# A vision tower on one core: padding copies, one weight load, PSUM bank sets and idle matmuls between the token rounds and the expert tiles

## The reference, cut to what matters

```
h   = tok(x, log_dt, B_ri, inv_A_real, A_imag)        # (16, 256, 512), complex exponentials, einsum
h   = concat(cls_tok, h)                              # (16, 257, 512)
u   = layernorm(layernorm(h)) ; gates = u @ W_in + b_in
s_t = (1-a_t) s_{t-1} + a_t b_t ; y = s * tanh(c)     # a = sigmoid(delta), scan over tokens
h   = h + y @ W_out + b_out + layernorm(h) @ W_skip + b_skip
x3  = layernorm(h)
scores = softmax(x3 @ gate_w) ; top 2 of 8 experts, weights comb
routed = sum_e comb_e * ((silu(x3 @ w_gate_e) * (x3 @ w_up_e)) @ w_down_e)      # hidden size 352
shared = (silu(x3 @ sw_gate) * (x3 @ sw_up)) @ sw_down                          # hidden size 704
h   = h + routed + shared
```

## Time and profile before

| | |
|---|---|
| median of 3 runs | 1160.75 us (1159.69 to 1163.04) |
| profiled execution, its own time | 1161.9 us |
| span in that execution | 1160.2 us |
| PE busy | 1068.6 us, 92% of the span |
| DVE, ACT, POOL busy | 812.9, 346.8, 381.5 us |
| mean granted PE clock | 0.968 |

### The profile page before, as it was taken

The page is one execution under the profiler, slowest core; times in us unless marked ns, Lnnn a source line. Parts: engine busy times, 40 slices in busy tenths (PEclk is TensorE's granted clock), DMA queues, the critical chain, the costliest instruction groups (busy, mean ns, idle before and its releaser), DMA issues.

```text
span 1160.2 us, 26590 instructions
## 1 busy us (share of the span) xinstructions
PE 1068.6 (92%) x7943; PEld 697.8 (60%) x7944; DVE 812.9 (70%) x2124; ACT 346.8 (30%) x659; POOL 381.5 (33%) x352
## 2 busy tenths in 40 slices
PE   3187899999999999999999998799999999999994
PEld 3055657766776677767776676355555555555552
DVE  7988998899889988898889655444444444444442
ACT  4422442344334443443334331111111111111110
POOL 1010132023212321232113211155555555655564
PEclk9588998999999999999999999899999999999998
DMA  8443445455553555455555985599999877787875
GB/s 288 132 149 102 123 119 173 129 149 161 177 166 110 166 176 159 122 157 182 155 139 148 287 285 189 135 181 200 178 201 165 135 127 132 133 131 129 134 120 75
DMA packets 305135, 183.32 MB, mean 158 GB/s; under 512 B 256098, under 2 KB 274914, under 8 KB 302900
## 3 DMA queue, kind: packets, MB, share of 16 engines
q1 hardware_dynamic: 288324, 136.38, 47.1%
q0 software_dynamic: 15504, 36.46, 15.7%
q10 hardware_dynamic: 1248, 9.72, 2.4%
HBM read 55.36 MB, written 79.47 MB: 116 GB/s over the span
## 4 chain that ended last, share of the span: by engine, by line
PE 75%; DVE 5%; DMA 4%; issue 2%; SPq 1%; ACT 1%; POOL 0%; POOLq 0%; DVEq 0%; ACTq 0%
PE bank L1001 28%; PE bank L1165 11%; PE bank L1175 11%; PE bank L1166 11%; PE bank L1080 7%; PE bank L1015 4%; DMA wexp<-x3w 1%; PE bank L1068 1%; PE bank L1084 1%; DMA x_slots<-x3w,sl 1%; DMA wexp<-w_halves 1%; DVE wexp L1381 1%; PE bank L1067 0%; PE bank L1066 0%; PE bank L1065 0%
## 5 line engine op out<-in xcount | busy, mean ns | idle before, releaser
L1001 PE MATMUL bank<-wexp 128*128 128x256 f16 (+2 forms) x3252 | 407.3, 286 | 10.4 <-issue 5.9
L1001 PEld LDWEIGHTS bank<-wexp 128*128 128x128 f16 x3252 | 310.5, 99 | 90.9 <-issue 16.0
L1165 PE MATMUL bank<-wexp,rows_in 128*128 x852 | 257.7, 315 | 10.8 <-issue 6.7
L1166 PE MATMUL bank<-wexp,rows_in 128*128 x852 | 257.3, 315 | 0.0
L1733 DVE SCALAR_TENSOR_TENSOR mixed<-bank,mixed 128x352 f32<-128x352 f32 x71 | 37.2, 524 | 163.4 <-ACT mixed L1338 160.7
L979 POOL DMA_INDIRECT out<-x2w,rows_in x70 | 111.8, 1597 | 119.4 <-DMA out<-x2w,rows_in 90.0
L933 POOL TENSOR_TENSOR inv<-var,power 128x4 f32<-128x4 f32 x17 | 29.2, 1715 | 362.1 <-DVE var L1563 362.1
L967 POOL TENSOR_TENSOR ex<-base,ld 128x8 f32<-128x8 f32 x71 | 120.7, 1700 | 76.1 <-DVE ld L1711 50.1
L1165 PEld LDWEIGHTS bank<-wexp,rows_in 128*128 128x128 f16 x852 | 83.6, 98 | 69.8 <-issue 28.8
L1338 ACT ACTIVATE mixed<-bank 128x352 f32<-128x352 f32 x71 | 32.9, 463 | 299.3 <-PE bank L1166 299.3
L1175 PE MATMUL bank<-wexp,gates 128*128 (+1 forms) x477 | 111.7, 379 | 3.5 <-DMA gates<-mixed 2.0
(11 more groups left out here) (289 smaller groups left out, 1271.9 us busy)
## 6 DMA issues: line engine op xcount, KB each, us to landing
w_halves<-rows_in SPq DMA_DIRECT2D x16, 704.0 KB, 4.7
wexp<-w_halves ACTq DMA_DIRECT2D x8, 1088.0 KB, 5.3
wexp<-w_halves SPq DMA_DIRECT2D x8, 1088.0 KB, 6.2
h_tok<-tokens SPq DMA_DIRECT2D x16, 512.0 KB, 2.7
mixed<-h_tok SPq DMA_DIRECT2D x32, 256.0 KB
out<-h SPq DMA_DIRECT2D x32, 256.0 KB
w_halves<-rows_in SPq DMA_DIRECT2D x16, 384.0 KB, 5.1
rows_in<-in_L_ffn_w_gate SPq DMA_DIRECT2D x16, 352.0 KB, 5.3
```

Source lines behind the costliest of these rows:

```text
L1001: last = MM(dst, stat_of(step, a), mov_of(step, b), start=(s_ == 0 and a + b == 0), stop=(s_ == len(steps) - 1 and a == 1))
L1165: MM(GB[:, 0:H], xT[b][:, a, c, :], wexp[:, u, o:o + H], start=s_, stop=e_)
L1166: last = MM(UB[:, 0:H], xT[b][:, a, c, :], wexp[:, u, o + H:o + 2 * H], start=s_, stop=e_)
```

## The change

Four edits, all between the end of the rounds and the tiles:

1. `pad_rows` is dealt anew: SP experts 0 to 3, ACT 4 and 5 (both ahead of its third silu), POOL 6 and 7 behind its last scatters, with a semaphore of their own (`c_zp`), for which SP waits too.
2. ACT's load of weight unit 7 (`first_weights(3)` in round 16) moves behind the two activations that follow it, and behind a wait for the router's matmuls of that round (`c_rt`).
3. `GB`, `UB` and `DB` become pairs of banks, taken in turn by tile; `gate_up(i)` waits for the `gx` of tile i-2, `down(i)` for the result of tile i-2.
4. PE runs eight matmuls of 512 columns with `zrow` (zeros) into `BY` between the last `shared_down` and the wait for tile 0.

```
-        GB, UB, DB = psum[1], psum[2], psum[5]
+        GB, UB, DB = (psum[1], psum[4]), (psum[2], psum[7]), (psum[5], psum[6])
...
+        c_zp = sem("c_zp")
...
-                        for e in range(5):
-                            pad_rows(sp, e)
+                        for e in range(4):
+                            pad_rows(sp, e, c_z)
                         sp.wait_ge(c_wo, 32 * NCH)
-                        sp.wait_ge(c_z, 16 * E)
+                        sp.wait_ge(c_z, 16 * 6)
+                        sp.wait_ge(c_zp, 16 * (E - 6))
...
+                    if isinstance(k, int) and k == LAST:
+                        gp.wait_ge(c_ri, 1)
+                        gp.wait_ge(c_pw, 64)
+                        for e in range(6, E):
+                            pad_rows(gp, e, c_zp)
+                            apart(gp, c_sep)
...
                     pe.wait_ge(d_xl[b], xcount(i, b))
-                    at_least(pe, d_gf, i)
+                    at_least(pe, d_gf, i - 1)
...
-                            MM(GB[:, 0:H], xT[b][:, a, c, :], wexp[:, u, o:o + H], start=s_, stop=e_)
+                            MM(GB[b % 2][:, 0:H], xT[b][:, a, c, :], wexp[:, u, o:o + H], start=s_, stop=e_)
...
-                    at_least(pe, d_ye, i)
+                    at_least(pe, d_ye, i - 1)
...
+                for i in range(8):
+                    MM(BY[:], ident16[:], zrow[:, 0:D], start=True, stop=True)
                 pe.wait_ge(d_tb, 1)
...
-                            pad_rows(act, 5)
+                            pad_rows(act, 4, c_z)
+                            pad_rows(act, 5, c_z)
                         silu(n, 2)
-                        if isinstance(k, int) and k == LAST:
-                            pad_rows(act, 6)
                         ghigh(n, 1)
                         first_weights(1)
                         silu(n, 3)
-                        if isinstance(k, int) and k == LAST:
-                            pad_rows(act, 7)
                         ghigh(n, 2)
...
-                    first_weights(3)
+                    if not (isinstance(k, int) and k == NCH):
+                        first_weights(3)
...
                         A(hdn[0:HK[2], 2, 0, :], rdn[0:HK[2], 2, :], ACT.Copy, scale=SW).then_inc(c_wh, 1)
+                    if isinstance(k, int) and k == NCH:
+                        act.wait_ge(c_rt, NCH + 1)
+                        first_weights(3)
```

More of the change, by code:

```diff
@@ L778, in vit_tower, with pad_rows @@
         xcount = lambda i, b: (i - b) * (32 // UNROLL) + 32
-        def pad_rows(eng, e):
+        def pad_rows(eng, e, done):
             turn = eng.value_load(roti[0:1, e:e + 1], min_val=0, max_val=P - 1)
             row = eng.value_load(runi[0:1, e:e + 1], min_val=0, max_val=ZERO - P)
-            eng.dma_start(xs_d[bass.ds(row, P), :], pads_d[e].rearrange("r q w -> (r q) w")[bass.ds(turn, P), :]).then_inc(c_z, 16)
+            eng.dma_start(xs_d[bass.ds(row, P), :], pads_d[e].rearrange("r q w -> (r q) w")[bass.ds(turn, P), :]).then_inc(done, 16)
         with nc.Block() as block:
@@ L1164, in gate_up @@
                             s_, e_ = (c == 0 and a + w == 0), (c == KD - 1 and a == 1)
-                            MM(GB[:, 0:H], xT[b][:, a, c, :], wexp[:, u, o:o + H], start=s_, stop=e_)
-                            last = MM(UB[:, 0:H], xT[b][:, a, c, :], wexp[:, u, o + H:o + 2 * H], start=s_, stop=e_)
+                            MM(GB[b % 2][:, 0:H], xT[b][:, a, c, :], wexp[:, u, o:o + H], start=s_, stop=e_)
+                            last = MM(UB[b % 2][:, 0:H], xT[b][:, a, c, :], wexp[:, u, o + H:o + 2 * H], start=s_, stop=e_)
                     last.then_inc(d_gu, 1)
@@ L1174, in down @@
                             o = UG + (c * 2 + w) * (D // 2)
-                            last = MM(DB[:], gT2[b % 4][0:HK[c], a, c, :], wexp[0:HK[c], bass.ds(unit, 2), o:o + D // 2],
+                            last = MM(DB[b % 2][:], gT2[b % 4][0:HK[c], a, c, :], wexp[0:HK[c], bass.ds(unit, 2), o:o + D // 2],
                                       start=(c == 0 and a + w == 0), stop=(c == KH - 1 and a == 1))
@@ L1337, in expert @@
                     act.wait_ge(d_gu, i + 1)
-                    A(sg[:], GB[:, 0:H], ACT.Silu, scale=SXW).then_inc(d_sg, 1)
+                    A(sg[:], GB[b % 2][:, 0:H], ACT.Silu, scale=SXW).then_inc(d_sg, 1)
                     act.wait_ge(d_gf, i + 1)
@@ L1727, in out_of @@
                         at_least(v, d_ys[b % 2], halfcount(i, b) - 16)
-                    TS(sums_of(i, b), DB[:], wv[:, b % 2:b % 2 + 1], 1.0 / SW, ALU.mult, ALU.mult).then_inc(d_ye, 1)
+                    TS(sums_of(i, b), DB[b % 2][:], wv[:, b % 2:b % 2 + 1], 1.0 / SW, ALU.mult, ALU.mult).then_inc(d_ye, 1)
                 def expert(i, b):
@@ L1732, in expert @@
                     at_least(v, d_gl, i)
-                    STT(gx[:], UB[:, 0:H], SXW, sg[:], ALU.mult, ALU.mult).then_inc(d_gf, 1)
+                    STT(gx[:], UB[b % 2][:, 0:H], SXW, sg[:], ALU.mult, ALU.mult).then_inc(d_gf, 1)
                     v.wait_ge(d_gh, i + 1)
```

## The result

| | before | after |
|---|---|---|
| median of 4 runs each | 1161.89 us (1159.69 to 1163.60) | 1155.74 us (1154.46 to 1158.06) |
| ratio, 95% interval | | 0.9942, 0.9923 to 0.9962 |
| profiled execution: its own time, span | 1161.9, 1160.2 us | 1158.06, 1156.6 us |

A forecast was written before the change was run, and what follows sets the result against it. PE carries most of the chain, so gains come where it stands still or runs at low clock. Start of tile 0 -2.9, from there to down(2) -4.9, together -7.8 against 1161.9: 1154.1, stated as 1153.5; own range 1151.5 to 1157.

The forecast's parts named there:

- Weights behind the router: At round 16's router: moving unit 7's load cuts PE's gap by 1.95 us and saves 1.6 of low clock, sum -3.6.
- I take the low stretch as gone too: Behind the router: with the gap at 1.4 us, the 3.4 us at 0.52 clock vanish, worth 1.6 us.
- Padding copies: Between room() and tile 0: the copies' release comes 2.9 us earlier, so tile 0 begins at 734.3.
- POOL becomes the last of the eight: Padding copies: POOL's second lands at 729.2, 2.6 us after SP's, making the release 2.9 us earlier rather than 5.5.
- my middle value: Landing of POOL's second padding copy: 729.2, taken as the middle between 725.9 and 732.6.
- Idle products: Before tile 0: eight matmuls of 1.7 us keep the clock, so tile 0 runs at full speed, saving 1.5 us.
- Bank sets: First tiles: bank pairs bring the end of down(2) from +30.9 to +26.0 us, gain 4.9, bounds 3.4 and 7.2.
- Gain 4.9, the 1.5 of tile 0's clock in it: Start of tile 0 to the end of down(2): 30.9 - 26.0 us, including 1.5 from tile 0 at full clock.
- both debts: First tiles: register loads start tile 2 at +8.0 to +9.4 instead of +7.2; down(0)'s transpose lands at +10.7 to +12.8.
- rival C: First tiles: banks give nothing beyond tile 0's clock, register loads and transposes being as late as gx; 1157.5 us, chance 0.1.
- later tiles have nothing to give: Tiles after down(2): no gain, pitch stays 5.5 us, and the tail hangs on the last tile's transpose as before.

The follow-up runs named there:

- after, once more: The changed kernel, nothing edited, timed again: 1159.55 us, ratio to before 0.9959.
- single banks: The changed kernel with one bank each for GB, UB and DB and the old waits: 1159.23 us, ratio to before 0.9954.
- late weight units: The changed kernel with SP's loads of weight units 8 to 15 at serve 8, 10, ... 22 instead of 1, 4, ... 22: 1160.56 us, 0.9958 of before.
- no idle products: The changed kernel without the eight idle matmuls before tile 0: 1160.25 us, ratio to before 0.9960.
- load in old place: The changed kernel with ACT's load of unit 7 back in its old place: 1163.52 us, ratio to before 0.9995.
- copies as before: The changed kernel with the padding copies dealt as before, SP five, ACT three, POOL none: 1162.07 us, ratio to before 0.9975.
- idle at the router: The changed kernel with six idle matmuls of 512 columns between the router halves of rounds 15 and 16: 1157.30 us, ratio to before 0.9931.
- pairs alone: The kernel before with only the bank pairs and their waits: 1164.51 us, ratio to before 0.9996.
- load moved alone: The kernel before with only the load of unit 7 moved behind the router: 1161.13 us, ratio to before 0.9966.
- load and copies: The changed kernel with neither bank pairs nor the idle matmuls before tile 0: 1160.27 us, ratio to before 0.9958.
- those, idle at the router: The kernel before with load moved, copies dealt anew and six idle matmuls between router halves of rounds 15 and 16: 1157.67 us, ratio to before 0.9936.
- old place, gap filled: The changed kernel with unit 7's load in its old place, six idle matmuls between router halves in round 15, fifteen in round 16: 1158.63 us, 0.9943 of before.

## Why the prediction was right, and where it wasn't

All traces from r0 on, in us, worked out from PE's rows in the order of time:

| kernel | t0 - r0 | `down(0)` - t0 | `down(3)` - t0 | `down(68)` - `down(3)` | low stretches, 650 to 780 us |
|---|---|---|---|---|---|
| before | 32.75 | 17.7 | 34.3 | 367.4 | 709, 736, 750 |
| after | 30.28 | 13.2 | 34.6 | 364.8 | 708 |
| after, once more | 30.28 | 15.2 | 31.7 | 365.9 | 676, 747 |
| single banks | 31.47 | 16.6 | 33.2 | 369.5 | 708, 749 |
| late weight units | 32.27 | 14.0 | 30.6 | 369.5 | 677, 711 |
| no idle products | 30.17 | 13.3 | 34.2 | 365.2 | 707 |
| load in old place | 33.78 | 15.8 | 32.4 | 366.5 | 678, 712, 753 |
| copies as before | 32.42 | 14.0 | 35.0 | 364.6 | 706, 737, 764 |
| idle at the router | 28.94 | 12.9 | 34.3 | 365.9 | none |
| pairs alone | 33.75 | 13.3 | 34.2 | 367.4 | 676, 711, 741 |
| load moved alone | 31.34 | 17.1 | 33.7 | 366.9 | 707, 748 |
| load and copies | 28.57 | 15.0 | 32.6 | 365.8 | 678 |
| those, idle at the router | 28.25 | 14.8 | 32.2 | 368.7 | none |
| old place, gap filled | 30.32 | 14.5 | 34.0 | 366.0 | none |

All traces have a low stretch again within their last 20 us, at the last tiles.

**Weights behind the router: gap right, clock wrong, and the largest part.** The transpose took 3.04 to 3.05 us in every trace with the load moved, 4.84 to 4.95 in those with it in its old place behind a plain gap, and the gap went from 3.37 to 1.46 us. That is the 1.95 of the prediction. The failed step is "I take the low stretch as gone too", because 1.42 us at 726 had cost no clock. The comparison was misread besides: the shortest gap that had lost the clock was not 2.45 us but the 2.2 before tile 2. In six of the eight traces with the gap of 1.46 us and no filler the clock fell behind round 16's router, and in the other two it had fallen behind round 15's, whose load I had not thought of. The two gaps of that length are not alike in what stands around them: at 726 it is matmuls of 512 columns, at the router twelve of 8 columns on either side, and I had compared the length alone. That this is the difference was not tested. Over many runs the clock still seems most of the move's gain (low 40.9 to 36.6, 4.3 us with an error of about 2, the worth of two to three such stretches), but the traces don't show where: the stretch behind round 16's router is there in all three with the old place and a plain gap and in six of the eight with the short gap. Single traces can't settle it, since before 650 us, in code that all kernels share, the low clock alone takes 24 to 32 us from trace to trace.

**Padding copies: start right, by another queue.** t0 came 2.5 us earlier from r0, where 2.9 was forecast, but not by the steps named. The end of `room()` came 1.9 earlier (718.82 - 704.42 = 14.4 before, 718.14 - 705.63 = 12.5 after) and not 3.6, since the clock stretch had stayed. From there SP issued its last copy after 8.0 us, against 10.0 for the fifth before, as the prediction had it. That copy landed 4.74 us later, not 3.26, which took 1.5 back: 1.9 + 2.0 - 1.5 = 2.4. "POOL becomes the last of the eight" failed: its issues took 0.60 and 0.51 us, the second began 1.44 behind the first, and both were out before SP's fourth, where I had put loads of 1.0 to 2.3 and issues of 0.96 to 1.54 per copy. But the landing of 6.3 us was near my upper bound of 6.86, so that POOL stayed only 0.6 us ahead.

The Trainium skill's rule that I had set against my middle value ("DMA: Bandwidth & Descriptors", "Issuing engines are not separate DMA queues") leaves a second issuing queue no cost of its own; this trace agrees as far as it goes, since SP's last copy landed 0.6 us behind POOL's. But the landings of all eight took 5.1 us in the median, where it had been 4.3. Timed, the new deal's share isn't shown to differ from nothing: 0.9975 without it against 0.9959, and 0.9958 with it against 0.9966.

**Idle products: no gain, and a price left open.** Tile 0 did start at full speed. But without them it did as well (1.54 us of waiting, clock 1.00), and the times are equal. Low stretches at tile 0 came only in traces with a wait of 2.18 us or more before it (2.45, 3.82, 2.18), and one with 2.94 had none there. The copies and the moved load had already made the wait short.

**Bank sets: the step that failed.** "Gain 4.9, the 1.5 of tile 0's clock in it" left 3.4 us for the pairs (with the low stretch at tile 2, some 1.6, in it, which the prediction didn't name). In the trace 4.5 us are there at `down(0)`, mostly clock; the end of `down(2)` comes at +30.15 where it was +30.9 and I had +26.0; at `down(3)` nothing is left. The timed pairs say the same: 0.9959 with and 0.9954 without, 0.9996 alone. I had foreseen both debts, the register loads and the late transpose, but too small. `down(0)` starts 13.2 us behind t0, outside my +10.7 to +12.8 for its transpose, and I had no wait before `down(2)`. In the repeat 2.6 us were left at `down(3)`, but t0 itself moves by up to 2 us (see below). Counted from SP's first load of rows, `down(3)` starts after 37.4 to 39.0 us in the eight traces with pairs and SP's weight loads in place, and after 36.2 to 38.9 in the five with single banks. PE's waits of the changed kernel from 690 to 775 us (total, times, longest):

```profile
PE bank L1173 <- issue: 3.2, 4, 1.3
PE bank L1183 <- DMA mixed<-mixed: 1.8, 1, 1.8
...
PE bank L1183 <- DMA gates<-mixed: 1.3, 1, 1.3
```

3.2 + 1.8 + 1.3 = 6.3 us of waits stand in the tiles, 5.4 of them before the end of `down(2)`, where I had counted on 2.3. The 1.8 is `down(0)`; SP issues its transpose 12.5 us behind its first load of rows (731.62), where it was 11.7 and in my sum, and the banks don't bring it forward:

```profile
744.11 2.29 SPq L895 DMA_TRANSPOSE mixed<-mixed  x1
```

The 1.3 is the transpose of 8.68 us, behind a weight load that SP had issued at 754.50 in the same queue; with those loads put off it didn't occur, nor did it in the repeat. So this is rival C's mechanism, whose chance I had as 0.1, with SP's queue as the larger part: register loads and transposes were as late as `gx`. What the Trainium skill ("TensorE: Matmul & The Clock Gate", "HAM oscillation — how this bites in real kernels") reports of one kernel, that PSUM double-buffering gave nothing further, agrees with the timed ratios here; my answer to it, that the waits before tiles 1 and 2 are there, was true and not enough, since others stand right behind them.

**Where the total came from then.** Of the 4.8 us by which the span is shorter from r0 on, 2.5 lie before tile 0, -0.3 in the first tiles, and 2.6 behind `down(3)`, where "later tiles have nothing to give". PE's waits for issue from 775 us to the end, before and then after:

```profile
PE bank L1165 <- issue: 4.5, 9, 1.2
```
```profile
PE bank L1173 <- issue: 2.3, 7, 0.7
```

That is 2.2 us less. Whether it is the pairs' doing, the traces don't settle: from `down(3)` to `down(68)` the eight kernels with pairs and SP's loads in place need 365.8 us in the mean (364.6 to 367.4), the five without pairs 367.7 (365.8 to 369.5). The spread within each (2.8 and 3.7) is larger than the 1.9 between them, and the timed ratios show none of it. The right total of this trace thus was in part luck, two errors that cancelled: 3.4 us for banks that gave none, and 2.6 us behind `down(3)` that I had not counted.

**What stays open.** With the idle products, PE's first row of tile 0 comes 4.05 to 4.29 us behind SP's first load in four of eight traces and 5.6 to 6.0 in the others; in all six without them it is 3.86 to 4.04. In the repeat of the changed kernel (PE in the order of time, then the chain):

```profile
733.82 1.90 PE L1205 MATMUL bank<-zrow,ident 128*128 128x512 f16 x8
...
737.05 0.32 PE L1173 MATMUL bank<-wexp,rows_in 128*128 x1 [1.33 <-DMA rows_in<-x_slots]
```
```profile
733.01 3.79 DMA rows_in<-x_slots
```

The chain puts it down to the landing of these rows, 3.79 to 4.16 us in the four late traces against 2.12 before; what slows it, and whether the eight matmuls have to do with it, isn't known. No experiment took it apart. One late trace stands without the pairs, so they aren't needed for it. Nor is it settled whether the pairs win or lose less than 2 us.

## What to carry to other kernels

A 1.1 MB load in another queue just ahead of a transpose that the bound engine waits for is worth moving: here 0.3%. The traces show the gap; the clock's part is seen in averages over many runs only. Put idle matmuls where the clock falls in the traces of several executions, not where one trace has a long wait: at the router they won 0.2 to 0.5% in three pairs of kernels with and without them (only the largest clear of noise by itself), before tile 0 no gain showed. Before giving an engine more buffers, look at what comes next behind the wait, its own register loads and the queue that feeds it; if that is as late, the gain is given back within a few steps.

## What the runs showed of the hardware that I had not expected

- A gap of 1.46 us between two groups of twelve 8-column matmuls was followed by a stretch near 0.5 in six of eight traces; gaps of 1.10 to 2.13 us at the router one round before in five of eleven. There the clock held behind gaps of 1.10 to 1.52 and fell behind those of 1.53 and more, but for one of 1.88; so longer gaps lose it more often, and length alone doesn't decide. With matmuls of 512 columns in the gap the clock fell in none of three, though the 8-column matmuls stood there as before. So it takes the gap; whether it also takes the narrow matmuls around it isn't shown. A stretch of 3.4 us at 0.52 costs 1.6 us.
- Filling the gaps doesn't reliably steady the time: the standard deviation of the span was 2.1 us in the changed kernel and 0.8 with its gaps filled, but 1.9 and 1.8 in the other two kernels with filled gaps.
- A plain DRAM-to-DRAM copy of 264 KB took POOL 0.5 to 0.6 us to issue, against 0.96 to 1.46 for a scatter of the rounds. POOL's second copy landed 6.3 us after its issue, SP's last 4.74. Four took SP's queue 6.73 us, five 9.72.
- A transpose issued 0.6 us behind a 1.1 MB load in the same queue landed after 8.68 us, and after 7.8 to 8.2 in four other traces; one behind such a load in another queue (1.4 us behind it in the kernel before) after 4.84 to 4.95, with that load moved after 3.04.
